# A routed mixture of experts in works of two sizes: split weights for 256 rows, unsplit fp32 weights for 128

## The reference, cut to what matters

```
gate = min(x @ W1[e], 10);  up = clip(x @ W3[e], -10, 10)
h = silu(gate) * up;        out_e = h @ W2[e]
result = shared(x) + sum over the two chosen experts e of weight_e * out_e
```

## Time and profile before

| what | value |
|---|---|
| median of 3 runs (lowest, highest) | 556.65 us (556.45, 556.83) |
| the profiled execution | 559.5 us, of which its span, first to last instruction, is 557.7 |
| mean granted clock of TensorE | 0.966 |
| busy PE, DVE, ACT, POOL | 512.2, 376.2, 256.9, 230.0 us |
| DMA | 65.03 MB, mean 117 GB/s |
| routed works on PE | from 125.56 to 309.01 us |

### The profile page before, as it was taken

How to read it: one execution, slowest core, us unless ns; L and a number is a source line. 1 busy time by engine, 2 the same in 40 slices (tenths; PEclk the granted TensorE clock), 3 DMA queues, 4 the chain that set the end, 5 groups by cost and what they waited for, 6 DMA issues and landing times.

```text
span 557.7 us, 9760 instructions
## 1 busy us (share of the span) xinstructions
PE 512.2 (92%) x3438; PEld 486.1 (87%) x3438; DVE 376.2 (67%) x893; ACT 256.9 (46%) x531; POOL 230.0 (41%) x194
## 2 busy tenths in 40 slices
PE   8699867989999999999999979999897788999996
PEld 7698866979999999999999869887675778999995
DVE  1574868656665666666664587699986766666665
ACT  0337572325544554445543225894750254354431
POOL 1402202746565666656666303487652200040300
PEclk9889998999999999999999979999897799999999
DMA  8760000946465776567672504000200200000001
GB/s 317 262 254 1 2 1 15 335 131 242 155 217 202 246 250 241 195 209 251 216 260 78 189 5 155 2 2 0 70 10 1 79 0 1 2 0 1 2 2 63
DMA packets 22922, 65.03 MB, mean 117 GB/s; under 512 B 6464, under 2 KB 15040, under 8 KB 20064
## 3 DMA queue, kind: packets, MB, share of 16 engines
q1 hardware_dynamic: 20480, 59.55, 31.0%
q0 software_dynamic: 2400, 4.93, 2.6%
HBM read 55.50 MB, written 8.97 MB: 116 GB/s over the span
## 4 chain that ended last, share of the span: by engine, by line
PE 59%; DVE 11%; DMA 3%; POOL 2%; issue 2%; ACT 2%; SPq 0%; DVEq 0%; POOLq 0%
PE psum L674 19%; PE psum L694 10%; PE psum L457 10%; PE psum L1091 4%; PE psum L474 3%; PE psum L1106 2%; PE psum L1123 2%; PE psum L1148 2%; PE psum L481 2%; DVE AT L2045 2%; PE psum L710 1%; DVE OW L2028 1%; DMA slots_out<-YO,XR 1%; DVE QK L2036 1%; PE psum L926 1%
## 5 line engine op out<-in xcount | busy, mean ns | idle before, releaser
L737 POOL TENSOR_TENSOR w0l<-stage,w0h 128x768 fp32r<-128x768 f32 x34 | 62.5, 1839 | 82.2 <-ACT w0h L721 66.9
L694 PE MATMUL psum<-w0d,a0h 128*128 128x192 f32 x492 | 84.2, 329 | 1.3 <-DVE a0h L776 1.3
L694 PEld LDWEIGHTS psum<-w0d,a0h 128*128 128x128 f32 x492 | 80.6, 192 | 1.6 <-DVE a0h L776 1.6
L769 DVE TENSOR_SCALAR a0t<-psum 128x256 f32<-128x256 f32 (+1 forms) x114 | 50.8, 445 | 39.3 <-PE psum L674 37.8
L748 ACT ACTIVATE psum<-psum 128x256 f32<-128x256 f32 x96 | 35.3, 368 | 85.2 <-PE psum L674 81.2
L674 PE MATMUL psum<-XWh,w0h 128*128 128x256 f32 x192 | 56.4, 294 | 0.0
L674 PE MATMUL psum<-XWh,w0t 128*128 128x256 f32 x192 | 54.7, 285 | 0.0
L674 PE MATMUL psum<-XWh,w0l 128*128 128x256 f32 x192 | 54.0, 281 | 0.0
L674 PE MATMUL psum<-XWl,w0h 128*128 128x256 f32 x192 | 53.9, 281 | 0.0
L674 PE MATMUL psum<-XWl,w0t 128*128 128x256 f32 x192 | 53.9, 281 | 0.0
L457 PE MATMUL psum<-X,w1h 128*128 128x384 f32 x144 | 49.6, 344 | 1.8 <-DVE a1hf L612 1.8
(11 more groups left out here) (264 smaller groups left out, 1280.3 us busy)
## 6 DMA issues: line engine op xcount, KB each, us to landing
stage<-moe0w SPq DMA_DIRECT2D x18, 1536.0 KB, 7.0
w0d<-moe0d SPq DMA_DIRECT2D x18, 576.0 KB, 4.0
stage<-moe1w SPq DMA_DIRECT2D x4, 1056.0 KB, 4.9
marked_rows<-zero SPq DMA_DIRECT2D x4, 772.0 KB, 13.2
XR<-marked_rows SPq DMA_DIRECT2D x16, 192.0 KB, 3.5
patch<-patches SPq DMA_DIRECT2D x3, 768.0 KB, 8.8
G<-slots_out SPq DMA_DIRECT2D x6, 288.0 KB, 4.6
patch<-patches SPq DMA_DIRECT2D x3, 384.0 KB, 5.5
```

The costliest lines, as they stand in the source:

```text
L694: last = nc.tensor.matmul(dst, A0["h"][qpar][:, fc, t * P:(t + 1) * P], W0[par]["down"][:, fc, :], start=(fc == these[0]), stop=(fc == the ...
L737: ins = engine.tensor_tensor(W0[par]["l"][:, mat, :], src, W0[par]["h"][:, mat, :].bitcast(F32), ALU.subtract)
L769: nc.vector.tensor_scalar(A0["t"][fc % 2][:, 0:width], bank[2 + fc % 2][:, 0:width], LIMIT, -LIMIT, ALU.min, ALU.max).then_inc(S0["clip_re ...
```

## The change

The routed rows are cut in parts of 128 slots. There are 25 of them at most, and always 17 works: eight wide ones (even numbers, two parts of one expert, computed as before) and nine small ones (odd numbers, one part). Each expert's pairs go to wide works, eight at most over all experts; what is left goes to the small ones. The two kinds alternate: 1 small, 2 wide, ..., 17 small.

In a small work the rows are not split: ACT copies the transposed rows to `XL`, which is stationary, and the gate and up weights stream unsplit, as fp32, straight out of `stage[1]`, in two halves of 384 columns (`e_rows_gate_up`, 8 matmuls in all, of which 4 have the last 64 rows). The hidden numbers then lie with the rows on the partitions, so PE transposes them (`e_turn`, 3 blocks for each half), ACT copies them (`e_turned`) and `e_down` runs on 128 rows. Splits are made for wide works alone, from `stage[0]`, which is single; the split results have two buffers. Work 2's low pieces are all DVE's, those of the others are three of POOL and one of DVE.

On DVE the numbers of the experts are made later, in three steps between the units of shared chunk 1, and a new step `places` behind the low pieces of work 2 gives each work the part at which its rows start; SP reads it for each row load, and waits for it once (`r_part`). The loads of SP come in another order, `marked_rows` has 27 x 128 slots and three zero stores in place of four, the results' list has no empty slots. At the end one unit of the tail stands ahead of the last down products, and the copy of the last result stands on DVE behind the products of three tail units. All loops over works are written out. The core of the diff:

```diff
-WT = 256
-
-WORKS = (PICKS * TOK - E0) // WT + E0
-SLOTS = WORKS * WT
+WT = P
+PARTS = (PICKS * TOK - E0) // WT + E0
+WIDE = E0
+LONE = PARTS - 2 * WIDE
+WORKS = WIDE + LONE
+SLOTS = (PARTS + 2) * WT
...
+        def low_engines(n):
+
+            return {0: "pppp", 2: "vvvv"}.get(n, "pppv")
...
             def load_weights(n):
-                if n >= 2:
-                    sp.wait_ge(S["w_lo"], 4 * (n - 1))
+                if n % 2 == 0:
+                    wait_lows(sp, n - 2)
+                elif n > 1:
+                    sp.wait_ge(S["gu_ready"], units(n - 1))
...
+            load_weights(2)
             load_weights(1)
             load_down(1)
+            sp.wait_ge(r_part, 1)
             sp.wait_ge(scattered, 16 * PICKS * TILES)
             load_rows(1)
             load_rows(2)
+            for n in range(1, WORKS + 1):
+                if n % 2:
+                    if n + 3 <= TAIL:
+                        load_weights(n + 3)
+                    if n + 2 <= WORKS:
+                        load_weights(n + 2)
+                        load_rows(n + 2)
+                    if n + 3 <= WORKS:
+                        load_rows(n + 3)
+                load_down(n + 1)
...
+        def e_rows_gate_up(pe, u, n):
+
+            pe.wait_ge(x_hi, n)
+            pe.wait_ge(ld_stage[1], staged(n))
+            w = W0[1]["stage"]
+            for half in range(2):
+                if n == 1:
+                    pe.wait_ge(S0["silu_ready"], u + (half - 1))
+                else:
+                    pe.wait_ge(S0["h_ready"], u + (half - 2))
+                pe.wait_ge(S0["clip_ready"], u + (half - 1))
+                cols = slice(half * LH, (half + 1) * LH)
+                for mat in range(2):
+                    dst = bank[2 * mat + half][:, 0:LH]
+                    nc.tensor.matmul(dst, XL[:, 0:WT], w[:, 2 * mat, cols], start=True, stop=False)
+                    last = nc.tensor.matmul(dst, XL[0:64, WT:2 * WT], w[0:64, 2 * mat + 1, cols], start=False,
+                                            stop=True)
+                last.then_inc(S0["gu_ready"], 1)
+
+        def e_turn(pe, u, n, half):
+
+            pe.wait_ge(S0["h_ready"], u + (half + 1))
+            if half:
+                pe.wait_ge(h_out, turned_in(n) - 1)
+            for k in range(3):
+                last = nc.tensor.transpose(bank[7][:, k * P:(k + 1) * P], hR[:, half * LH + k * P:half * LH + (k + 1) * P],
+                                           ident)
+            last.then_inc(h_T, 1)
...
+        def e_turned(act, n, half):
+
+            act.wait_ge(h_T, turned_in(n) - 1 + half)
+            if not half:
+                act.wait_ge(S0["down_ready"], downs(n - 2) if n > 2 else 6)
+            nc.scalar.activation(hT[:, 3 * half:3 * half + 3, :], bank[7][:, 0:LH].rearrange("p (k t) -> p k t", t=P),
+                                 ACT.Copy).then_inc(h_out, 1)
...
+            for n in range(1, WORKS + 1):
+                u = units(n)
+                if n % 2:
+                    e_rows_gate_up(pe, u, n)
+                    if n < WORKS:
+                        e_rows(pe, n + 1)
+                    e_turn(pe, u, n, 0)
+                    if n > 1:
+                        e_down(pe, units(n - 1), 0, n - 1, 0, False, loaded(n - 1))
+                        e_turn(pe, u, n, 1)
                 else:
+                    e_gate_up(pe, u, n, 0, None, range(1))
+                    if n == 2:
+                        e_turn(pe, units(1), 1, 1)
+                    e_gate_up(pe, u, n, 0, None, range(1, FC0))
+                    e_rows(pe, n + 1)
+                    e_down(pe, units(n - 1), 1, n - 1, 1, False, loaded(n - 1))
+            e_gate_up(pe, TAIL_U, TAIL, 0, 2, range(AHEAD, AHEAD + 1))
+            e_down(pe, units(WORKS), 1, WORKS, 1, False, loaded(WORKS))
+            e_gate_up(pe, TAIL_U, TAIL, 0, 2, range(AHEAD + 1, FC0))
+            e_down(pe, TAIL_U, 0, TAIL, 0, True, loaded(TAIL), range(AHEAD, FC0))
...
+SPLIT_AT = (1, 2, 4, 5)
...
+            for n in range(1, WORKS + 1):
+                u = units(n)
+                if n % 2:
+                    e_rows_silu(act, u, 0)
+                    e_rows_silu(act, u, 1)
+                    if n < WORKS:
+                        e_rows_high(act, n + 1, units(n))
+                    e_turned(act, n, 0)
+                    if n > 1:
+                        e_turned(act, n, 1)
+                else:
+                    e_act(act, u, 2 * WT, these=range(1))
+                    if n == 2:
+                        e_turned(act, 1, 1)
+                    for fc in range(1, FC0):
+                        if fc in SPLIT_AT:
+                            e_split_act(act, n + 2, SPLIT_AT.index(fc))
+                        e_act(act, u, 2 * WT, these=range(fc, fc + 1))
+                    e_rows_high(act, n + 1, units(n))
+            e_act(act, TAIL_U, CHW, these=range(AHEAD, FC0))
+...
+            def places():
+
+                own.step(nc.vector.scalar_tensor_tensor(out=shift2[:, 1, :], in0=wide_from, scalar=-2.0, in1=base[:],
+                                                        op0=ALU.mult, op1=ALU.add))
+                own.link(nc.vector.scalar_tensor_tensor(out=shift2[:, 0, :], in0=twos[:], scalar=2.0, in1=base[:],
+                                                        op0=ALU.mult, op1=ALU.add))
+                own.link(nc.vector.tensor_tensor(shift2[:, 0, :], shift2[:, 0, :], lone_from, ALU.subtract))
+                own.link(reached(within, 1))
+                own.link(nc.vector.tensor_tensor(within, within, above, ALU.subtract))
+                here = within.rearrange("p (k w e) -> p k w e", k=2, e=E0)
+                own.link(nc.vector.tensor_reduce(held[:], here, AX.X, ALU.add))
+                own.link(nc.vector.tensor_tensor(here, here, shift2[:].unsqueeze(2).to_broadcast(grid), ALU.mult))
+                own.link(nc.vector.tensor_reduce(place[:], here, AX.X, ALU.add))
+                own.link(nc.vector.tensor_tensor(held[:], held[:], order[:], ALU.mult))
+                own.link(nc.vector.tensor_tensor(place[:], place[:], held[:], ALU.add))
+                nc.vector.tensor_scalar(part[:], place[:], float(PARTS), None, ALU.add).then_inc(r_part, 1)
...
-            experts()
             e_product(dve, 0, 0, 5, CHW)
-            e_dve(dve, FC0, 1, CHW, None, None, None)
-            e_split_low(nc.vector, dve, 1, 1)
+            e_dve(dve, FC0, 1, CHW, None, {1: wide_parts, 2: lone_parts, 3: experts})
+            e_split_low(nc.vector, dve, 2)
+            places()
             prior()
             share(sc, E0, comb[:], True)
             weights()
             for t0, t1, at in SHARED_ADD[0:3]:
                 e_acc(dve, t0, t1, at, t1)
-            e_dve(dve, 2 * FC0, 0, CHW, 3, None, None, these=range(AHEAD))
-            e_rows_low(dve, 1, 1)
+            e_dve(dve, 2 * FC0, 0, CHW, 3, these=range(AHEAD))
             for t0, t1, at in SHARED_ADD[3:5]:
                 e_acc(dve, t0, t1, at, t1)
-            e_dve(dve, units(1), 1, WT, 6, None, None, {3: lambda: e_rows_low(dve, 2, 0)})
-            e_dve(dve, units(2), 0, WT, 9, (3, 1), lambda: e_copy(dve, 1, 1, None))
-            e_dve(dve, units(3), 1, WT, 11, (4, 0), lambda: e_copy(dve, 2, 0, None))
-            e_dve(dve, units(4), 0, WT, 13, (5, 1), lambda: e_copy(dve, 3, 1, 32))
-            with dve.Fori(0, (WORKS - 6) // 2, 1) as i:
-                e_dve(dve, i * 12 + units(5), 1, WT, i * 4 + 15, (i * 2 + 6, 0), lambda: e_copy(dve, i * 2 + 4, 0, i * 32 + 32))
-                e_dve(dve, i * 12 + units(6), 0, WT, i * 4 + 17, (i * 2 + 7, 1), lambda: e_copy(dve, i * 2 + 5, 1, i * 32 + 64))
-            e_dve(dve, units(WORKS - 1), 1, WT, 2 * WORKS + 3, (WORKS, 0), lambda: e_copy(dve, WORKS - 2, 0, 16 * WORKS - 64))
-            e_dve(dve, units(WORKS), 0, WT, 2 * WORKS + 5, None, lambda: e_copy(dve, WORKS - 1, 1, 16 * WORKS - 32))
-            e_copy(dve, WORKS, 0, 16 * WORKS - 32)
-            e_dve(dve, TAIL_U, 1, CHW, 2 * WORKS + 7, None, None, these=range(AHEAD, FC0))
+
+            for n in range(1, WORKS + 1):
+                u = units(n)
+                if n % 2:
+                    if n > 2:
+                        dve.wait_ge(h_T, turned_in(n - 2))
+                    else:
+                        dve.wait_ge(S0["down_ready"], 6)
+                    for half in range(2):
+                        e_rows_product(dve, u, half)
+                else:
+                    e_dve(dve, u, 0, 2 * WT, downs(n - 2))
+                if n % 2 and n < WORKS:
+                    e_rows_low(dve, n + 1)
+                if n % 2 == 0:
+                    e_split_low(nc.vector, dve, n + 2)
+                if n > 1:
+                    e_copy(dve, n - 1)
+            e_dve(dve, TAIL_U, 0, CHW, downs(WORKS - 1), these=range(AHEAD, FC0 - 1))
+            e_copy(dve, WORKS)
+            e_dve(dve, TAIL_U, 0, CHW, None, these=range(FC0 - 1, FC0))

...
```

(47 more changed lines are left out.)

366 lines of the change are left out of this document (191 added, 175 removed).

## The result

The changed kernel takes **562.57 us** (median of four, 561.66 to 564.51) against 556.55 of the kernel before in the same runs (median of four): 1.0107 times as long, 95% interval 1.0067 to 1.0146. It is slower, and outside the forecast range. Two more comparisons, each with the kernel before beside it on the same chip, gave 1.0149 (1.0105 to 1.0193) and 1.0104 (1.0069 to 1.0139). The profiled execution has a span of 562.7 us and took 564.51.

The account below looks back on a forecast made before the run. PE was taken to bound the routed works: 21.9 us less there, against +6.6 start, +1.4 and +0.5 first pair, +1.9 and +3.15 end, sum -8.35 from 556.65, gave 548.3 us; range 541.5 to 555.5.

Parts of the forecast that it names:

- I take 5.01, the nearest in form: Small works' fp32 gate/up on PE: 16 records of 384 columns at 0.313 us, the down products' rate, 5.01 us a work.
- The half-empty second matmul of 64 rows is counted in full: Small works' gate/up on PE: the second matmul, with only 64 rows, was priced like a full one.
- My upper bound of 5.6 a work: Small works' gate/up: at most 0.70 us per 384 columns from L1106's fp32 matmuls, 5 us more over nine works.
- Rival D: Small works' gate/up: fp32 streams slower, 5.0 us, and 16 turns between forms cost 3.2: 556.5 us, no change; chance 0.05.
- The wide works: Eight wide works on PE keep their form and 11.45 us each, 91.6 us in all.
- The steady pair hides the rest: Routed works: PE's 19.2 us a pair covers ACT, DVE, POOL and the loads, so no stall.
- B: Wide works: POOL delays the stage buffer, 0.7 us in each of seven pairs, 5 us in all: 553.3 us; chance 0.18.
- C: Wide works: the one stage buffer becomes the bound with 12 us loads, 2.9 us late in seven pairs: 568.6; chance 0.08.
- The start: Before the routed works: later expert numbers, load and DVE queue make them begin at 132.2 instead of 125.56, +6.6 us.
- The first pair: First wide gate/up waits for the second half's product and the rows' low copy, +1.4 us; half clock in fp32, +0.5.
- The end: After the routed works: a tail unit ahead of the last downs, +1.9 us; last copy behind three tail products, +3.15.
- What follows Y: The kernel's part after Y is ready: forecast as unchanged.

## Why the prediction was wrong

- **The failed step** is "I take 5.01, the nearest in form". L694's rate holds for products that all have 128 rows: without turns of height the same gate/up measured 5.16 (the 0.15 above 5.01 because records of 192 columns in a row start 0.163 apart; 0.157 divides a stretch at whose end the next matmul follows sooner). As the change has it, it measured 6.62: nine works by 1.61 are 14.5 us, more than the whole forecast gain of 8.35. The prediction put nothing for the eight changes of height. "The half-empty second matmul of 64 rows is counted in full" sounded like the safe side, but the rows it leaves empty cost the turns. My upper bound of 5.6 a work, from the earlier trace rows, was below the measured value too; those four matmuls all have 96 rows and hold no turn.
- **Rival D** had the right direction and the wrong mechanism: it priced turns between fp32 and the split form, two a pair. The turns that cost are between heights inside the fp32 products, eight a work. That its 0.2 us a turn is near the 0.18 measured is luck.
- **The wide works** were mis-sized the other way: five of the seven steady ones take 6.90 us for 7.25, two take 7.16. That is some 2.2 us less over the eight; why they got faster was not tried.
- **The steady pair hides the rest**: right. No idle PE in steady state, ACT, DVE, POOL and the loads all covered; B and C did not come about. Seven pairs take 20.74 each where 19.22 was forecast; 1.61 more for the small gate/up and 0.28 less for the wide one make 20.55, and 0.2 a pair, 1.3 us over seven, stay spread over small products.
- **The start**: mechanism right at each point (numbers at 103.0, load at 104.04, places behind the low pieces, transposes released by DVE's additions, down products by a0h); +5.1 instead of +6.6. The load landed in 7.6 us, between the 9.8 and the 6.4 of the earlier trace rows. The Trainium skill's rule (DMA: Bandwidth & Descriptors, Queues, rings and completion order) that descriptors are consumed in ring order had pointed to 6.4; this trace agrees in part. By the load (2.2) and 0.5 more, DVE's chain released PE's down products 2.7 us earlier than forecast, and they gave 1.2 of it back: they took 4.0 us, at a granted clock of 0.50, not the 2.85 of before, at 0.64.
- **The first pair**: +1.4 and +0.5 forecast. It took 149.47 - 130.65 = 18.82 us; the steady pair behind it less its missing 3.76 is 16.90, so 1.92. Right, the wait for `XWl` being 1.1 us and the half clock in the first product 0.7.
- **The end**: the copy behind three tail products, PE idle 6.9 us, Y 17.9 us after the last down for 17.2. Right to 0.7 us.
- **Together**: Y came 12.6 us later than forecast (327.31 for 314.71). 14.5 - 2.2 - 1.5 (start) + 0.7 (end) + 1.3 (the rest of seven pairs) = 12.8. What follows Y grew by 0.75 us where nothing was forecast, most of it the transposes at half clock. The two profiled executions are thus 5.0 us apart; the medians are 6.0, and the 1.0 between is not placed.

So the change as such, fp32 weights streaming past stationary rows, does what it says; the order at the start, the order at the end and the 64-row products gave its gain away. With all three mended it is 14 us faster than the kernel before beside it, and of the 21 to 22 us by which it then beats the changed kernel, 13 come from the operand made full height, 2.6 to 4.4 from the start and the rest from the end.

## What to carry to other kernels

A rate read from uniform matmuls holds only for uniform ones: where stationary operands of different heights alternate, count the turns and price them, or give all products one height, even if that means computing rows twice with a scale. When a change moves a late load or a result copy, write down the queue of the engine that consumes it: what is independent of the load goes ahead of it, and a copy that starts a long way home goes ahead of products that nobody awaits yet.

## What the runs showed of the hardware that I had not expected

A change between 128 and 64 stationary rows in fp32 cost 0.17 to 0.19 us, in three arrangements (4, 8 and 16 turns a work). Which step inside PE it is was not tried, nor whether other heights or types pay the same.

On two of the four chips of the experiments all eight profiled executions show PE idle without a visible wait, 5.8 to 8.5 us between 107 and 120 us, and the kernel before took 565.7 us beside them; on the other two none of eight does, and it took 556. It comes while the marked rows are scattered, and persists where the DMA engines are otherwise nearly idle. PE's signals are late with it: in all eight the trace ends two groups of PE's down products between 105.3 and 115.0 us, and the semaphore events for both come together, at 119.3 to 120.4; in the other eight each comes 0.02 us behind its matmul. The queue that the profile names "instruction" brings one packet of 16 KB in this stretch, at 116 to 122 us with the idle and at 108 to 111 without it, after about as many down records of PE (33 to 38, and 29 to 43). So a lack of instructions is argued at most, and what holds PE and its signals was not found.

It is not known whether the kernel before has the idle there, since it was not profiled on such a chip; its 9.7 us more would fit. Whether moving the scatter would help stays open too. For comparisons it means that ratios of different chips don't mix: the order at the start is worth 2.6 to 5.2 us where the idle is absent and nothing where it shows.
